# A ViT tower on one Trainium2 core: undivided probabilities and a column of ones in the 16-column attentions

## The reference, cut to what matters

```python
a = softmax(q @ k.T * 0.25 (+ bias))      # 36 x 36 for each of 12 heads
o = a @ v                                 # 36 x 16
out = concat_heads(o) @ w_proj + b_proj   # 192 -> 192
```

## Time and profile before

| what | value |
| --- | --- |
| time, median of 3 runs | 906.39 us (905.71 to 907.11) |
| profiled execution, own time | 909.75 us |
| its span | 908.0 us |
| PE busy | 831.0 us (92%) |
| DVE, ACT, POOL busy | 543.1, 461.0, 410.3 us |
| second attention, first scores to last mix | 301.1 to 436.6 us |
| third attention, first scores to last mix | 549.3 to 681.1 us |

### The profile page before, as it was taken

One profiled execution on the slowest core, in us unless ns is written; L12 is line 12 of the kernel. 1 busy time (PEld: TensorE's weight loads), 2 busy tenths in 40 slices (PEclk: granted clock), 3 DMA queues, 4 the chain that ended last, 5 costly groups with the idle time before them and its releaser, 6 DMA issues. The chain is left out here.

```text
span 908.0 us, 20892 instructions
## 1 busy us (share of the span) xinstructions
PE 831.0 (92%) x7511; PEld 748.5 (82%) x7511; DVE 543.1 (60%) x1466; ACT 461.0 (51%) x1150; POOL 410.3 (45%) x489
## 2 busy tenths in 40 slices
PE   9899999999998798998999988988979999999982
PEld 8889998899997577776999986776757899899972
DVE  2236555556665788884773326888875622466645
ACT  0346565555644587874345526877735221255533
POOL 1535444344444444432441225777851355244445
PEclk9989999999999999996999998999969999999997
DMA  9810111111110131214400002633200011233243
GB/s 315 255 50 21 22 35 37 31 31 30 38 36 2 33 67 25 37 19 123 74 1 1 1 26 42 138 68 68 42 7 2 29 62 63 76 103 100 83 149 116
DMA packets 103940, 55.75 MB, mean 61 GB/s; under 512 B 67264, under 2 KB 94512, under 8 KB 103840
## 3 DMA queue, kind: packets, MB, share of 16 engines
q1 hardware_dynamic: 98032, 43.04, 19.9%
q0 software_dynamic: 3792, 7.84, 2.5%
q10 hardware_dynamic: 2016, 3.54, 1.3%
HBM read 29.81 MB, written 13.97 MB: 48 GB/s over the span
## 5 line engine op out<-in xcount | busy, mean ns | idle before, releaser
L931 POOL TENSOR_TENSOR attn_prob<-attn_prob,attn_recip 100x432 f32<-100x432 f32 x64 | 58.6, 915 | 75.5 <-DVE attn_recip L1310 75.2
L450 POOL TENSOR_TENSOR attn_prob_x<-attn_prob,attn_recip 100x864 f32<-100x864 f32 x32 | 52.7, 1646 | 52.7 <-DVE attn_recip L759 52.7
L1886 POOL DMA_INDIRECT results<-moe_hid_shared x43 | 41.3, 960 | 58.4 <-ACT moe_hid_shared L2101 58.4
L1596 ACT ACTIVATE mlp_hid<-psum,columns 128x384 f32<-128x384 f32 x72 | 38.1, 579 | 41.4 <-PE psum L96 41.4
L1060 PEld LDWEIGHTS psum<-attn_prob_t,attn_values 108*64 108x64 f32 x1024 | 39.3, 142 | 13.6 <-ACT attn_prob_t L1179 7.8
L1060 PE MATMUL psum<-attn_prob_t,attn_values 108*64 108x36 f32 x1024 | 41.6, 228 | 6.1 <-ACT attn_prob_t L1179 4.1
L2076 ACT ACTIVATE moe_silu<-psum 128x384 f32<-128x384 f32 x36 | 17.7, 491 | 56.6 <-PE psum L107 56.6
L1033 PE MATMUL psum<-attn_keys_a,attn_q_a 128*64 128x288 f32 x256 | 45.8, 437 | 0.0
L1043 PE MATMUL psum<-ident,attn_prob 100*108 100x100 f32 x256 | 35.8, 265 | 9.5 <-POOL attn_prob L931 9.5
L1172 ACT ACTIVATE attn_prob<-attn_prob 100x432 f32<-100x432 f32 x64 | 36.5, 571 | 15.5 <-POOL attn_prob L938 14.7
L1305 DVE TENSOR_REDUCE attn_row_sum<-attn_prob 100x12 f32<-100x432 f32 x64 | 38.0, 594 | 8.1 <-ACT attn_prob L1172 7.9
(11 more groups left out here) (473 smaller groups left out, 2853.5 us busy)
## 6 DMA issues: line engine op xcount, KB each, us to landing
embed_patches<-in_x SPq DMA_DIRECT2D x8, 768.0 KB, 17.2
sorted_rows<-mlp_pad_zeros SPq DMA_DIRECT2D x1, 4214.0 KB, 15.7
moe_hid_shared<-sorted_rows SPq DMA_DIRECT2D x43, 98.0 KB, 2.0
attn_v<-attn_v_tok SPq DMA_DIRECT2D x16, 216.0 KB
attn_values<-attn_v_tok SPq DMA_DIRECT2D x96, 27.0 KB
side_raw_a<-in_w_gu_dram SPq DMA_DIRECT2D x8, 288.0 KB, 3.3
side_raw_b<-in_w_gu_dram SPq DMA_DIRECT2D x16, 144.0 KB, 3.4
h_rows<-results SPq DMA_DIRECT2D x6, 288.0 KB, 5.3
```

What stands on the lines that cost most here:

```text
L450: nc.gpsimd.tensor_tensor(prob_x[k % 2][:, :, :, :], prob[k % 3][:, :, :].rearrange("p h (a n) -> p h a n", a=1) .to_broadcast([QP, HEADS, ...
L931: nc.gpsimd.tensor_tensor(pr, pr, recip[k % 2][:, :].rearrange("p (h a) -> p h a", a=1) .to_broadcast([QP, HEADS, SEQ]), ALU.mult).then_in ...
L1596: nc.scalar.activation(hid_step(n), bank(n % 3)[:, 0:MW], ACT.Gelu, bias=b_up[:, c:c + 1]).then_inc(S["gelu_done"], 1)
L1886: nc.gpsimd.indirect_dma_start(out=results, out_offset=bass.IndirectOffsetOnAxis(ap=x_in[j % x_ring][:, D:D + 1].bitcast(U32), axis=0), in ...
```

## The change

The probabilities are no longer divided before they are mixed. `sum_up` (DVE) and `normalise` (POOL) go. The values of each head get a 17th column of ones (HW = 17), so the mix gives each head's sum beside its 16 values. The operands of the mix are exchanged: `prob_t` is now the weights (64 token columns for image 0, 36 for image 1), the values are the moving operand (51 columns, three heads), and the result has tokens on partitions, 204 columns. DVE's new `norm_z` takes the reciprocals of the 12 sums from PSUM and multiplies the 204 columns. PE's new `turn_z` transposes them, 102 columns at a time, into bank 5; ACT copies them to `z_t`, now 102 partitions. The rows of the output weights are laid out to match, and the bias row is row 16, since a sum divided by itself is 1.

In the pipeline everything behind the exponential moves up one step: `turn(k - 1)`, `mix(k - 2)`, then `turn_z(k - 2)` in the same step, DVE's `norm_z(k - 2)` in that step too, and `copy_z(k - 3)` as before. Probability buffers are two instead of three, the turn has one PSUM bank instead of two, and the ring of `z_t` is nine tiles.

The diff, cut to its core:

```diff
+HW = 17
+ZC = HEADS * HW // 2
...
-    z_ring = 3 * P
+    z_ring = 9 * P
...
-    values_bd = [sb(f"values{p}", [3 * SEQ, 8, 4 * 64]) for p in range(2)]
-    prob = [sb(f"prob{p}", [QP, HEADS, SEQ]) for p in range(3)]
+    values_bd = [sb(f"values{p}", [3 * SEQ, 8, HEADS * HW]) for p in range(2)]
+    prob = [sb(f"prob{p}", [QP, HEADS, SEQ]) for p in range(2)]
...
-        def normalise(k):
-            pool.wait_ge(S["recip_ready"], k + 1)
-            pr = prob[k % 3][:, :, :]
-            nc.gpsimd.tensor_tensor(pr, pr, recip[k % 2][:, :].rearrange("p (h a) -> p h a", a=1)
-                                    .to_broadcast([QP, HEADS, SEQ]), ALU.mult
-                                    ).then_inc(S["normalised"], 1)
...
-            nc.gpsimd.memset(values_bd[p][0:SEQ, :, 48:49], 1.0).then_inc(S["values_cleared"], 1)
+            pool.wait_ge(S["values_cleared"], 4 * p + 1)
+            ones = values_bd[p][:, :, :].rearrange("p i (m j e) -> p (i m) j e", j=3, e=HW)[:, :, :, 16]
+            nc.gpsimd.memset(ones, 1.0).then_inc(S["values_cleared"], 1)
+            pool.wait_ge(S["values_cleared"], 4 * p + 2)
+            nc.gpsimd.affine_select(out=ones, in_=ones, compare_op=ALU.is_ge, fill=0.0, base=0,
+                                    pattern=[[0, 32], [-SEQ, 3]], channel_multiplier=1
+                                    ).then_inc(S["values_cleared"], 1)
...
-            if 1 <= k <= units:
-                normalise(k - 1)
...
         def turn(k):
-            pe.wait_ge(S["normalised"], k + 1)
-            if k >= 2:
-                pe.wait_ge(S["turned_copied"], k - 1)
+            pe.wait_ge(S["exp_done"], k + 1)
+            if k >= 1:
+                pe.wait_ge(S["turned_copied"], k)
...
             if k >= 1:
+                pe.wait_ge(S["z_normed"], k)
+            for n in range(4):
+                both = prob_t[k % 2][:, n, :, :].rearrange("p a q -> p (a q)")
+                for a in range(2):
+                    i = 2 * u + a
+                    v = values_bd[g % 2][:, 3 * (i % 3) + i // 3, 3 * HW * n:3 * HW * (n + 1)]
+                    toks, to = (slice(0, 64), slice(0, 64)) if a == 0 else (slice(SEQ, UNIT), slice(64, QP))
+                    last = nc.tensor.matmul(z_ps[to, 3 * HW * n:3 * HW * (n + 1)], both[:, toks], v,
+                                            start=True, stop=True)
+            last.then_inc(S["mixed"], 1)
+
+        def turn_z(k):
+            pe.wait_ge(S["z_normed"], k + 1)
+            if k >= 1:
                 pe.wait_ge(S["z_copied"], k)
...
+            flat = z_tok[k % 2][:, :, :].rearrange("p h e -> p (h e)")
+            for c in range(2):
+                last = nc.tensor.transpose(bank(5)[0:ZC, c * P:c * P + QP], flat[:, c * ZC:(c + 1) * ZC],
+                                           ident[0:QP, 0:QP])
+            last.then_inc(S["z_turned"], 1)
...
-            if k >= 3:
-                mix(k - 3)
+            if 2 <= k < units + 2:
+                mix(k - 2)
...
+            if 1 <= k <= units:
+                turn(k - 1)
             if 2 <= k < units + 2:
-                turn(k - 2)
+                turn_z(k - 2)
...
-            if 2 <= k < units + 2:
-                copy_turned(k - 2)
+            if 1 <= k <= units:
+                copy_turned(k - 1)
...
-        def sum_up(k):
-            dve.wait_ge(S["exp_done"], k + 1)
-            dve.wait_ge(S["recip_ready"], k)
-            nc.vector.tensor_reduce(row_sum[:, :], prob[k % 3][:, :, :], axis=AX.X, op=ALU.add
-                                    ).then_inc(S["sum_ready"], 1)
-            dve.wait_ge(S["sum_ready"], k + 1)
+        def norm_z(k):
+            dve.wait_ge(S["mixed"], k + 1)
+            z = z_ps[0:QP, :].rearrange("p (h e) -> p h e", h=HEADS)
+            nc.vector.reciprocal(recip[k % 2][:, :], z[:, :, 16]).then_inc(S["recip_ready"], 1)
+            dve.wait_ge(S["recip_ready"], k + 1)
             if k >= 2:
...
+                dve.wait_ge(S["z_turned"], k - 1)
+            nc.vector.tensor_tensor(z_tok[k % 2][:, :, :], z, recip[k % 2][:, :].rearrange("p (h a) -> p h a", a=1)
+                                    .to_broadcast([QP, HEADS, HW]), ALU.mult).then_inc(S["z_normed"], 1)
...
-            if 1 <= k <= units:
-                sum_up(k - 1)
+            if 2 <= k < units + 2:
+                norm_z(k - 2)
```

More of the change, by code:

```diff
@@ L949, in clear @@
             nc.gpsimd.memset(values_bd[p][:, :, :], 0.0).then_inc(S["values_cleared"], 1)
-            pool.wait_ge(S["values_cleared"], 2 * p + 1)
-            nc.gpsimd.memset(values_bd[p][0:SEQ, :, 48:49], 1.0).then_inc(S["values_cleared"], 1)
+            pool.wait_ge(S["values_cleared"], 4 * p + 1)
[5 more added lines that the diff above has]
+                                    ).then_inc(S["values_cleared"], 1)
+            pool.wait_ge(S["values_cleared"], 4 * p + 3)
+            nc.gpsimd.affine_select(out=ones, in_=ones, compare_op=ALU.is_ge, fill=0.0, base=SEQ - 1,
+                                    pattern=[[0, 32], [SEQ, 3]], channel_multiplier=-1
+                                    ).then_inc(S["values_cleared"], 1)
         clear(0)
@@ L1052, in mix @@
             if k >= 1:
-                pe.wait_ge(S["z_copied"], k)
-            ps = z_ps
-            for a in range(2):
-                i = 2 * u + a
-                v = values_bd[g % 2][:, 3 * (i % 3) + i // 3, :].rearrange("p (n m) -> p n m", n=4)
-                for n in range(4):
-                    r = 64 * (n % 2)
-                    last = nc.tensor.matmul(ps[r:r + 64, n // 2, a * SEQ:(a + 1) * SEQ], v[:, n, :],
-                                            prob_t[k % 2][:, n, a, :], start=True, stop=True)
-            last.then_inc(S["mixed"], 1)
+                pe.wait_ge(S["z_normed"], k)
[11 more added lines that the diff above has]
+            if k >= 1:
+                pe.wait_ge(S["z_copied"], k)
+            flat = z_tok[k % 2][:, :, :].rearrange("p h e -> p (h e)")
[3 more added lines that the diff above has]
+            last.then_inc(S["z_turned"], 1)
         def project_out(t):
@@ L1068, in project_out @@
             w_o = out_ws[t * len(out_ws) // NT]
-            nc.tensor.matmul(out_ps, z_t[:, 0, z_cols(t)], w_o[:, 0, :], start=True, stop=False)
-            nc.tensor.matmul(out_ps, z_t[:, 1, z_cols(t)], w_o[:, 1, :], start=False, stop=True
+            nc.tensor.matmul(out_ps, z_t[:, 0, z_cols(t)], w_o[0:ZC, 0, :], start=True, stop=False)
+            nc.tensor.matmul(out_ps, z_t[:, 1, z_cols(t)], w_o[0:ZC, 1, :], start=False, stop=True
                              ).then_inc(S["out_done"], 1)
@@ L2757, in vector @@
                     n = 2
-                    for i, kept, rows_ in ((1, D // 2, P), (2, D // 3, 80)):
+                    for i, kept, rows_ in ((1, D // 2, P), (2, D // 3, 4 * HW)):
                         dve.wait_ge(S_w, n)
@@ L2878, in by_group @@
         v = np.asarray(v)
-        out = np.zeros((2, 2, 4, 16) + v.shape[1:], v.dtype)
-        out[:, :, 0:3] = v.reshape((2, 2, 3, 16) + v.shape[1:])
-        return out.reshape((2, P) + v.shape[1:])
+        out = np.zeros((2, P) + v.shape[1:], v.dtype)
+        heads = v.reshape((2, HB, 16) + v.shape[1:])
+        for h in range(HB):
+            out[:, HW * h:HW * h + 16] = heads[:, h]
+        return out
     def narrow_columns(w):
```

45 lines of the change are left out of this document (20 added, 25 removed).

## The result

The changed kernel takes 927.21 us (925.50 to 929.87 in 4 runs), the kernel before 906.44 us: a ratio of 1.0223, 95% interval 1.0203 to 1.0244. That is 20.8 us slower; forecast were 12.8, with a range of 902 to 929.

The account below looks back on a forecast made before the run. TensorE's queue was taken as the time in both 16-column attentions. Groups 12.4, late values 2.3 and 3.4, ends -5.5 and POOL's clearing 0.2 sum to +12.8 us on 906.39: 919 us, range 902 to 929.

Parts of the forecast that it names:

- Groups: Four-unit groups of both 16-column attentions: 1.0 us longer each in the second, 0.9 in the third, 12.4 us together.
- a floor under the 1.0, not an addition: Values' DMAs in each group: ready 1.4 us late for the earlier mix, not added to the group's 1.0 us.
- First steps: A group's first step: TensorE waits 0.63 us for DVE's multiply before turning the heads, net 0.4 us.
- Third steps: A group's third step: the turn waits 0.5 us for ACT's exponential, behind four key masks; net 0.4 us.
- Two late spreads: Values late at the third attention's start, +2.3 us, and in the group whose issues took 11.07 us, +3.4 us.
- Turns and mix: TensorE, each unit: two added turns cost 0.18 us, 11.5 over 64 units; the mix's 51 columns cost nothing.
- the ends: Last units of both attentions: shorter chains without POOL's pass and DVE's sum, -1.5 us in the second, -4.0 in the third.
- I count 2.5 of that wait as going: Third attention's end: of the turn's 3.18 us wait for POOL, behind a long DVE pass, 2.5 us go.
- the round trip: TensorE's mix, DVE's reciprocal and multiply, TensorE's heads' turn in one step: 16 first steps at 0.1 to 1.2 us.
- the base: The +12.8 us from profiles was set on the median 906.39; the profiled execution, 909.75, lay 3.36 above it.
- The fast rival: Both attentions: 18.8 us of waits vanish, new ones hide, turns add 11.5; 899 us, chance 0.16.
- The rival of DVE late in every round: The 0.63 us wait for DVE also met in 32 rounds where it was hidden: 939 us, chance 0.13.

Follow-up runs that it names:

- run 1: The changed kernel with the turn of a unit's heads moved on TensorE from its step's end to behind the next unit's scores: 921.22 us, ratio 1.0160.
- run 5: The changed kernel with the turn of a unit's heads a step later, behind the next mix: 924.17 us, ratio 1.0193.
- run 3: The kernel before with two idle turns of 102 columns added ahead of each unit's four turns: 911.98 us, ratio 1.0040.
- run 6: The changed kernel with the heads' turn a step later behind the next mix, and a group's first mix waiting for six of nine DMAs: 907.43 us, ratio 1.0012.
- run 12: The kernel before without POOL's division and DVE's sum and reciprocal, the turn waiting for the exponential instead: 891.47 us, ratio 0.9845.
- run 8: The kernel before with two idle turns of 102 columns a unit between a unit's scores and the mix: 910.95 us, ratio 1.0059.

## Why the prediction was right, and where it was wrong

The direction and the mechanism were right: work removed beside TensorE bought little in the groups, two turns and a chain over DVE inside the step cost more, and the values came too late. The size was short by 8.0 of 20.8 us; 927.21 lies 2 us inside the range's upper end.

- *Groups.* 1.0 us a group was forecast for the second attention, 1.14 measured; the third lost 7.7 us where 8.8 was forecast. The loop of the values was called "a floor under the 1.0, not an addition". Its length was forecast well (8.7 us from issue to mix, 8.8 to 8.95 measured; 4.2 to the values, 3.97), and it is a floor: runs 1 and 5 took the waits for DVE away and the two middles together did not shrink (192.1 and 192.3 us against 191.7). What the prediction did not name is that the move of the mix put this loop next to the group's length, at 15.0 us instead of 11.4.
- *First steps.* 0.63 us of wait for the multiply was worked out, 0.52 measured.
- *Third steps.* The turn was to wait 0.5 us for the exponential in each. The second attention's middle has no such wait; there, in four of the six groups, the mix of the same step waits 0.5 to 0.7 us for the DMAs. The third attention's middle has four waits for the exponential, 1.6 us in all. For the second the size was right by luck, since the releaser was another.
- *Two late spreads.* 2.3 us in the third attention's first group came to 2.8. (The mix waits 2.84 us for the DMAs there; before, it waited 1.24 for the copied probabilities.) In the group of the long issues 4 us of wait were expected and 1.94 came: the nine issues took 8.87 us, not 11.07, and they no longer met the large weight loads in the same way. That group grew by 2.8 us (18.61 against 15.85), but 2.0 of it are busy time of PE (16.15 against 14.17), part of it turns and part the granted clock, 0.91 over the group where it was 1.00 before; the idle time grew by 0.8. That the sum of these groups came near is partly luck.
- *Turns and mix.* Two turns cost 0.18 us where they stand (341.62 to 341.80), sixteen mix records 0.55 us with 51 columns. Run 3 shows that the turns' 11.5 us are no 11.5 us of time: 3.6, as long as old waits can take them up.

**The step that failed** is the ends. "I count 2.5 of that wait as going", for a DVE pass of 3.18 us: it did not go. The pass still takes 2.53 us, and other waits stand beside it. In the changed kernel's end, the timelines of DVE, POOL and PE show:

```profile
681.42 2.53 DVE L1341 TENSOR_SCALAR h_rows<-h_rows,attn_mean_var,attn_rstd 128x192 f32<-128x192 f32 x1
683.88 0.59 DVE L1302 TENSOR_TENSOR attn_prob<-psum,bias 100x432 f32<-100x432 f32 x1
684.50 0.60 DVE L1306 TENSOR_REDUCE attn_row_max<-attn_prob 100x12 f32<-100x432 f32 x1
685.02 0.22 DVE L1317 RECIPROCAL attn_recip<-psum 100x12 f32<-100x12 f32 x1
685.28 0.37 DVE L1321 TENSOR_TENSOR attn_z_tok<-psum,attn_recip 100x204 f32<-100x204 f32 x1
```

```profile
681.04 0.91 POOL L934 TENSOR_TENSOR attn_prob<-attn_prob,attn_row_max 100x432 f32<-100x432 f32 x1 [1.02 <-DVE attn_row_max L1306]
681.89 0.58 POOL L2611 MEMSET w_gu_b_lo<- 128x576 f32 x1
682.43 1.41 POOL L2613 TENSOR_TENSOR w_gu_a_lo<-side_raw_a,w_gu_a_hi 128x576 fp32r<-128x576 f32 x1
```

```profile
685.71 0.38 PE L1073 MATMUL psum<-ident,attn_z_tok 100*102 100x100 f32 x2 [1.95 <-DVE attn_z_tok L1321]
```

DVE's pass ends at 683.95, 0.1 us after POOL's run of three operations (682.43 + 1.41 = 683.84). The long partner, last in that run, is the splitting of the experts' weights, which the change doesn't touch, and not the division of the probabilities that it removes. Whether the two meet hangs on when the pass begins: in run 6 it begins inside POOL's run and takes 2.53 us again, in run 12 it begins 0.16 us ahead of it (651.14) and takes 0.37 us. It fits the Trainium skill, SBUF — State Buffer, section "Who interferes with whom": a VectorE tensor_scalar in a two-port mode and GpSimd exclude each other; the mode itself stands in no trace. The multiply stands behind that pass on DVE, and the turn of the heads behind the multiply, in the same step. PE waits six times for the multiply in the 29.97 us, 7.0 us in all, 1.95 of them behind this pass; before, it waited 5.7 us for the division there. Run 12 shows what was to be had there (9.0 us), run 1 that moving the turn gets 7.0 of it back, at a granted clock of 1.00 in place of 0.83. I had dropped two links of the chain and not counted that the round trip, priced for first steps, stands in the end's chain too. That is 4.1 of the 4.5 us by which the sum fell short. The rest nearly cancels: 1.5 us behind the experts' first matmul, at a granted clock of 0.96 against 0.98 (its cause is open), 0.9 and 0.5 in the second attention's groups and the third's first, against 1.1 in the third's other groups and 1.4 in the small stretches.

Of the other 3.5 us between forecast and median, 3.2 are the base: before's profiled execution lay 3.36 us above its median, after's 0.16 above its own, and I set a difference between profiles on the median. The last 0.3 is time outside the spans.

The fast rival is refuted for this kernel. Its 899 us would have been near all the same, with both terms too large: without the division the kernel gains 14 us (run 12) where it had 18.8, and the turns alone cost 3.6 (run 3) where it had 11.5. What it lacked was the pipeline's step. Moving everything one step up, which shortened nothing, spent the slack of the spread and put DVE's round trip into the step. The rival of DVE late in every round is refuted by its waits: 27 for the multiply, in 64 units.

## What to carry to other kernels

Where a stage gains an engine round trip, try giving it a pipeline step instead of taking one away: here the same arithmetic took 927 us with the mix and the turn in one step, 902 with everything behind the exponential a step later, 7.7 us of it in a stretch where the granted clock differed too. Before crediting a wait that disappears, name the partner of the long pass ahead of it, and follow the new chain through the ends as well as through a group. When a move changes which step waits for a transfer, add up the loop around that wait (issue to landing, wait to producer, producer to issue) before and after. When a repair gives little, look at the loop around the next wait: if it is as long as the period, two repairs are needed, and neither can be judged alone.

## What was not expected of the hardware

A turn's price hangs on its neighbours. In run 1 it stands between scores and mix, both of 64-column tiles; PE's timeline there:

```profile
355.75 0.41 PE L1036 MATMUL psum<-attn_keys_b,attn_q_b 128*64 128x144 f32 x4
356.10 0.38 PE L1073 MATMUL psum<-ident,attn_z_tok 100*102 100x100 f32 x2
356.41 0.67 PE L1063 MATMUL psum<-attn_values,attn_prob_t 108*64 108x51 f32 x16
357.00 0.40 PE L997 MATMUL psum<-ring_a_hi,w_qkv_a_hi 128*128 128x288 f32 x1
```

In run 5 it stands behind the mix, ahead of full tiles:

```profile
357.32 0.41 PE L1036 MATMUL psum<-attn_keys_b,attn_q_b 128*64 128x144 f32 x4
357.57 0.62 PE L1063 MATMUL psum<-attn_values,attn_prob_t 108*64 108x51 f32 x16
358.12 0.38 PE L1073 MATMUL psum<-ident,attn_z_tok 100*102 100x100 f32 x2
358.27 0.38 PE L997 MATMUL psum<-ring_a_hi,w_qkv_a_hi 128*128 128x288 f32 x1
```

The same matmuls take 1.25 us there and 0.95 here: 0.30 us a unit with the order changed and nothing else, more than the 0.18 that the turns were costed at. The middles of runs 3 and 8 say the same (4.5 and 6.4 us for 24 units). The Trainium skill, TensorEngine Tiling (Array Packing), section "Key Properties", states that changing the tiling mode drains TensorE; by that, run 1 changes it twice more a unit, and the rows agree, without showing the drain itself.
